# Layer 3's head normalisation as tensor_scalar pieces on two engines in a new order of tasks, and another path for the softmax denominators of layers 0 to 2

## The chip, the cores and the metric

The kernel runs on one core of one Trainium2 chip. The metric is the device time of one execution in microseconds (us), taken as the median of several runs. PE, DVE, ACT and POOL are the engines TensorE, VectorE, ScalarE and GpSimd; SP issues the DMAs.

## The reference, cut to what matters

The reference is a network of four layers on x (16 batches of 128 tokens, 256 wide) with a context of the same shape. Each layer is an attention and then a feed-forward part. The attentions of layers 0 to 2 differ in projections and heads (16 of width 8, 8 of width 16, 32 of width 8), but each is

```
scores = q @ k / sqrt(width)
prob   = softmax(scores, axis=-1)
out    = prob @ v            # the division by the softmax's sum may come last
```

Layer 3's attention has two passes: tokens over themselves ("own") and tokens over the context ("cross"). Each has 16 query heads and 8 key and value heads of width 128. Queries and keys are normalised head by head before the scores:

```
mu  = mean(x, -1); var = mean(square(x - mu), -1)
x   = (x - mu) * rsqrt(var + EPS) * w + b
```

and the concatenated output is rounded to FP8 values before the output projection.

## The kernel before, in words

The stages run one after the other: attention of layer 0 (`a0`), its feed-forward, attention of layer 1 (`a1`), and so on. The engines of a stage are separate programs that meet only at semaphores, and each runs its own list in program order.

**Attentions of layers 0 to 2** (class `Attention`, names `a_...` in the profile). The scores are computed twice from bf16 stacks `qs` and `ks`: `pe_first` (L326) gives them to `dve_max` (L476), which takes the row maxima; `pool_split` (L432 to L439), a turn on PE (L372) and a DMA (L513) put the maxima into reserved rows of the stack; `pe_second` (L344) gives scores less maximum to ScalarE's exponential (`act_exp`, L383). `pe_apply` (L361) multiplies by the values. The value tile has a column of ones behind each head's columns, so that PSUM row `HD` of each block of 32 rows holds the softmax's denominator. ScalarE copies a bank to `osb` (L412). Work is ordered by ticks: in tick g every engine does what `pair_at(g, offset)` and `batch_at(g, offset)` give it; two batches are a pair of 2W ticks (16, 8 and 8 in layers 0, 1 and 2). The tail of pair q is counted from `DONE`: at DONE the SP queue stores `osb` with all its 32 rows per block to DRAM (`od`, L517); at DONE+4 it waits for that and gathers the denominators (`zc`, L522) and the outputs (`oc`, L525, four DMAs or in layer 1 two); at DONE+7 VectorE takes the reciprocal (L482) and SP stores it (`zd`, L531); at DONE+9 SP spreads it (`zr`, L536); at DONE+12 GpSimd multiplies (`on`, L424); then PE projects in layers 0 and 2 (L701, L1035), and VectorE adds to X (L771, L902, L1092).

At a stage's start VectorE clears the stacks with memsets (`dve_clear`, L458, L461), and GpSimd presets `edge`, `mx` and `vt` (`pool_preset`, L444 to L449) ahead of all its ticks. Layer 0's VectorE program then has its constants (L743 to L755), whose last result (`bias_ready`) PE awaits before its first projection. SP's `sp_edges` waits for the clearing, and the stack DMAs (L502, L507) stand behind it in SP's queue.

**Layer 3** (class `Layer3Pass`; `a3o_` own, `a3x_` cross). Every engine runs its tasks of one list, `OWN_ORDER` or `CROSS_ORDER`, per batch. A step works on four batches at once: "a" attends, "c" centres and turns the heads, "p" projects, "r" prepares the next. A batch has 24 heads of 128 elements. ScalarE copies projections to `raw` (L2705), VectorE takes `bn_stats` (L2801) and derives mean and variance (`deviation`, L2807 to L2818), GpSimd raises to the power -1/2 (`inverse`, L2517, L2519) and centres the heads in six units of four (`center`): one 128x512 subtraction of a broadcast mean (L2525), a drain, one 128x512 multiplication (L2529). PE turns a unit (`turn_heads`, L2615) after the semaphore `centered`. VectorE also has the maxima of the scores (L2822), `normalise` (L2826, L2829), the rounding of the output (`round_task`, L2242 to L2246, L2838, L2842) and, in the own pass, the rounding of the input.

Of the kernel before, what the change touches and what calls it, by code (L numbers as in the profile page):

```python
# [12 lines left out]
F32 = mybir.dt.float32  # L13
# [9 lines left out]
P = 128  # L23
# [147 lines left out]
class Attention:  # L171
# [5 lines left out]
    def __init__(self, nc, st, X, name, heads, width, n, halves, scale, lead, stacks, values):  # L177
# [38 lines left out]
        self.od = nc.dram_tensor(f"{name}_od", (B // 2, 4, 32, G * 2 * D), F32, kind="Internal").ap()  # L216
# [7 lines left out]
        self.cleared = sem("cleared")  # L224
# [54 lines left out]
    def stacks_in(self, engine, q, dmas):  # L279
        engine.wait_ge(self.stack_in[q % self.SB], 16 * dmas * (q // self.SB + 1))  # L280
# [120 lines left out]
    def act_outputs(self, act, b, i):  # L401
        act.wait_ge(self.av_done, self.QUADS * b + (i + 1) * self.BANK_QUADS)
        q = b // 2
        if q >= 2 and b % 2 == 0 and i == 0:
            act.wait_ge(self.od_in, 16 * (q - 1))
# [14 lines left out]
    def pool_divide(self, pool, q):  # L420
        pool.wait_ge(self.zr_in[q % 2], 16 * (q // 2 + 1))
        pool.wait_ge(self.oc_in[q % 2], 16 * self.G * (q // 2 + 1))
        wait(pool, self.added, q)
        self.nc.gpsimd.tensor_tensor(self.on[:, :, :], self.oc[:, q % 2, :, :], self.zr[:, q % 2, :, :],  # L424
                                     ALU.mult).then_inc(self.on_ready, 1)

    def pool_split(self, pool, b):
# [3 lines left out]
        wait(pool, self.turned, b)  # L431
        self.nc.gpsimd.tensor_copy(self.mx[:, :, :, 0, :], raw).then_inc(self.split_step, 1)  # L432
# [9 lines left out]
    def pool_preset(self, pool):  # L442
        nc = self.nc
        nc.gpsimd.memset(self.edge[:, 0, :], 0.0).then_inc(self.preset, 1)  # L444
        nc.gpsimd.memset(self.edge[:, 1, :], -1.0).then_inc(self.preset, 1)
        nc.gpsimd.memset(self.mx[:, :, :, :, :], 0.0).then_inc(self.preset, 1)
# [38 lines left out]

    def sp_edges(self, sp):

        if self.HALVES == 1:
            sp.wait_ge(self.cleared, 1)
            return  # L490
        sp.wait_ge(self.cleared, 2)
        sp.wait_ge(self.preset, 2)
        out = self.maxima_slots(self.ks[:, :, :, :, :]).rearrange("p s t b n -> p (s t) (b n)")
        sp.dma_start(out, self.edges(1, out)).then_inc(self.edge_in, 16)

    def edges(self, k, out):
        return self.edge[0:8, k, :].unsqueeze(1).broadcast_to(list(out.shape))

    def sp_clear_maxima(self, sp, q):

        out = self.maxima_slots(self.qs[:, q % self.SB, :, :, :]).rearrange("p t b n -> p t (b n)")
# [13 lines left out]
    def sp_store_outputs(self, sp, q):  # L515
        sp.wait_ge(self.o_taken, 2 * self.QUADS // self.BANK_QUADS * (q + 1))
        sp.dma_start(self.od[q].rearrange("j r n -> (j r) n"), self.osb[:, q % 2, :, :, :]).then_inc(self.od_in, 16)  # L517

    def sp_gather_outputs(self, sp, q):
        sp.wait_ge(self.od_in, 16 * (q + 1))  # L520
        wait(sp, self.zd_in, 16 * (q - 1))
        sp.dma_start(self.zc[0:32 * self.G, q % 2, :], self.od[q, :, self.HD]).then_inc(self.z_in, 16)  # L522
        wait(sp, self.on_ready, q - 1)
        for k in range(self.G):
            sp.dma_start(self.oc[k:P:self.G, q % 2, :, :].rearrange("p b n -> p (b n)"),  # L525
                         self.od[q, :, 0:self.HD, 2 * k * D:2 * k * D + 2 * D].rearrange("j d n -> d j n")
                         ).then_inc(self.oc_in[q % 2], 16)

# [4 lines left out]
    def sp_spread_reciprocal(self, sp, q):  # L533
        sp.wait_ge(self.zd_in, 16 * (q + 1))
        rows = 4 * self.G
        sp.dma_start(self.zr[:, q % 2, :, :], self.zd[q].rearrange("(h n) -> h n", n=2 * D).unsqueeze(0).broadcast_to(  # L536
            [P // rows, rows, 2 * D])).then_inc(self.zr_in[q % 2], 16)
# [16 lines left out]
def stage_l0_attention(nc, dram, X):  # L554
    with Stage(nc, "a0") as st:
# [29 lines left out]
        with nc.Block() as block:  # L585
# [24 lines left out]
            def _(pool):  # L610
                a.pool_preset(pool)
                for g in a.ticks():
                    if (b := a.batch_at(g, LEAD + W)) is not None:
# [26 lines left out]
                    if (q := a.pair_at(g, DONE + 12)) is not None:  # L640
# [92 lines left out]
            def _(dve):  # L733
                a.dve_clear()

# [21 lines left out]
                dve.wait_ge(a.preset, a.presets())  # L757
                for g in a.ticks():
# [7 lines left out]
                    if (q := a.pair_at(g, DONE + 7)) is not None:  # L766
# [8 lines left out]
def stage_l1_attention(nc, dram, X):  # L775
    with Stage(nc, "a1") as st:
# [8 lines left out]
        with nc.Block() as block:  # L785
# [24 lines left out]
            def _(pool):  # L810
                a.pool_preset(pool)
                for g in a.ticks():
                    if (b := a.batch_at(g, LEAD + W)) is not None:
# [17 lines left out]
                    if (q := a.pair_at(g, DONE + 12)) is not None:  # L831
# [74 lines left out]
def stage_l2_attention(nc, dram, X):  # L906
    with Stage(nc, "a2") as st:
# [20 lines left out]
        with nc.Block() as block:  # L928
# [2109 lines left out]
```

## Time and profile before

| | |
|---|---|
| median of 3 runs | 3255.49 us (3253.8 to 3255.79) |
| the profiled execution | 3247.69 us, its span 3245.9 us |
| PE, DVE, ACT, POOL busy | 74%, 58%, 41%, 34% of the span |
| attention of layer 0 | about 16 to 349 us of the span |
| attention of layer 1 | about 514 to 705 us |
| attention of layer 2 | about 1064 to 1308 us |
| layer 3, own and cross | about 1547 to 2170 and to 2701 us |

Times of rows are microseconds from the span's start. A busy share is an average over stages with different limits; the waits within a stage say what sets its pace.

### The profile page before, as it was taken

Reading aid. Unit: us, or ns where it says so; the run is one execution under the profiler, and the core shown is the slowest. Engines: PE = TensorE matmul, PEld = TensorE weight load, DVE = VectorE, ACT = ScalarE, POOL = GpSimd, SP = SyncE. Lnnn points to the kernel's source line nnn. Section 1 sums busy time; section 2 is a strip of 40 time slices with the busy share of each in tenths; the row PEclk is TensorE's granted clock in tenths of the full one; section 3 lists DMA queues with packets and bytes.
Section 4 is the critical chain, followed back from the end, with each engine's and each line's share of the span. In section 5 each row is a group of like instructions: output and inputs, shape, how many; then the busy total and the mean of one; then the engine's idle time right before and its main releaser. Section 6 shows DMA issues by size and latency. Waiting matters only on the chain. (4 is left out here: it accounts for less than half of the span.)

```text
span 3245.9 us, 45398 instructions
## 1 busy us (share of the span) xinstructions
PE 2403.6 (74%) x14854; PEld 1747.9 (54%) x14906; DVE 1870.1 (58%) x3551; ACT 1324.1 (41%) x3059; POOL 1102.8 (34%) x991
## 2 busy tenths in 40 slices
PE   3887143855988477499278788867888984899997
PEld 2332021423556333477166666646777764778776
DVE  3775586645453354333588888857788775332332
ACT  0666151730200155111367667656666761111110
POOL 5432004510002342210367667527656650500000
PEclk9999565986989688599699999989999996899999
DMA  3342102522300234100200000020000001200001
GB/s 88 93 112 84 47 0 77 146 87 97 154 7 1 72 103 135 49 4 1 92 1 0 0 0 0 1 73 5 4 5 3 4 1 63 65 1 1 1 1 26
DMA packets 83598, 138.04 MB, mean 43 GB/s; under 512 B 19760, under 2 KB 63216, under 8 KB 78192
## 3 DMA queue, kind: packets, MB, share of 16 engines
q1 hardware_dynamic: 83440, 135.99, 13.4%
q8 instruction: 92, 1.51, 0.2%
q14 instruction: 66, 0.54, 0.1%
HBM read 76.64 MB, written 23.72 MB: 31 GB/s over the span
## 5 line engine op out<-in xcount | busy, mean ns | idle before, releaser
L476 DVE TENSOR_REDUCE a_mraw<-a_first_ps 128x4 f32<-128x1024 f32 (+1 forms) x256 | 309.2, 1220 | 126.4 <-PE a_first_ps L326 126.1
L383 ACT ACTIVATE a_et<-a_second_ps 128x1024 f32<-128x1024 f32 x256 | 262.4, 1025 | 160.1 <-PE a_second_ps L344 158.2
L1425 DVE TENSOR_TENSOR f3e_gated<-f3e_silu,f3e_u_ps 128x512 f32<-128x512 f32 x96 | 66.0, 687 | 305.4 <-PE f3e_s_ps L1376 203.3
L1406 ACT ACTIVATE f3e_silu<-f3e_g_ps 128x512 f32<-128x512 f32 x96 | 57.4, 598 | 397.4 <-PE f3e_g_ps L1363 397.4
L1385 PE MATMUL f3e_y_ps<-f_w,f3e_hidden 128*128 128x256 f32 x768 | 181.4, 380 | 1.9
L361 PE MATMUL a_o_ps<-a_et,a_vt 128*32 128x256 f32 x2048 | 167.6, 400 | 10.4 <-ACT a_osb L412 9.0
L344 PE MATMUL a_second_ps<-a_qs,a_ks 64*128 64x256 bf16 (+2 forms) x896 | 117.4, 297 | 58.6 <-ACT a_et L383 54.6
L1385 PEld LDWEIGHTS f3e_y_ps<-f_w,f3e_hidden 128*128 128x128 f32 x768 | 146.6, 191 | 18.4 <-DVE f3e_hidden L1428 1.2
L326 PE MATMUL a_first_ps<-a_ks,a_qs 64*128 64x256 bf16 (+2 forms) x1280 | 122.5, 266 | 32.1 <-DVE a_mraw L476 17.7
L2655 PE MATMUL a3o_o_ps<-a3o_wparts,a3o_catq 128*128 128x256 bf16 x768 | 111.0, 302 | 36.9 <-DVE a3o_catq L2842 36.5
L344 PEld LDWEIGHTS a_second_ps<-a_qs,a_ks 64*128 64x128 bf16 (+1 forms) x896 | 42.1, 96 | 157.8 <-ACT a_et L383 123.5
L2525 POOL TENSOR_TENSOR a3o_raw<-a3o_raw,a3o_mu 128x512 f32<-128x512 f32 x96 | 120.7, 1258 | 4.0 <-issue 2.7
L2696 ACT ACTIVATE a3x_weights<-a3x_s_ps,a3x_nmax 128x128 f32<-128x128 f32 x256 | 91.4, 379 | 63.0 <-DVE a3x_nmax L2822 63.0
L2529 POOL TENSOR_TENSOR a3x_raw<-a3x_raw,a3x_dev 128x512 f32<-128x512 f32 x96 | 111.1, 1157 | 14.3 <-issue 1.5
L2525 POOL TENSOR_TENSOR a3x_raw<-a3x_raw,a3x_mu 128x512 f32<-128x512 f32 x96 | 112.5, 1171 | 4.4 <-issue 3.2
L2655 PEld LDWEIGHTS a3o_o_ps<-a3o_wparts,a3o_catq 128*128 128x128 bf16 x768 | 80.6, 109 | 60.3 <-DVE a3o_catq L2842 45.3
L2529 POOL TENSOR_TENSOR a3o_raw<-a3o_raw,a3o_dev 128x512 f32<-128x512 f32 x96 | 105.0, 1094 | 13.6
L1345 POOL CAST f_w_high<-f_w_raw 128x512 fp32r<-128x512 f32 x36 | 25.0, 695 | 237.2 <-SPq L1324 218.9
L326 PEld LDWEIGHTS a_first_ps<-a_ks,a_qs 64*128 64x128 bf16 (+1 forms) x1280 | 70.9, 100 | 60.2 <-DVE a_mraw L476 26.7
L2696 ACT ACTIVATE a3o_weights<-a3o_s_ps,a3o_nmax 128x128 f32<-128x128 f32 x256 | 92.0, 388 | 27.6 <-DVE a3o_nmax L2822 26.8
L2577 PE MATMUL a3x_p_ps<-a_wkv,a3x_ctx_parts 128*128 128x512 f32 x384 | 102.9, 411 | 0.0
L2655 PE MATMUL a3x_o_ps<-a3x_wparts,a3x_catq 128*128 128x256 bf16 x768 | 96.8, 277 | 7.6 <-DVE a3x_catq L2842 7.6
(540 smaller groups left out, 6564.8 us busy)
## 6 DMA issues: line engine op xcount, KB each, us to landing
f_w<-in_f_w SPq DMA_DIRECT2D x16, 1216.0 KB, 8.7
a_qs<-a_parts SPq DMA_DIRECT2D x144, 128.0 KB, 2.4
a_od<-a_osb SPq DMA_DIRECT2D x16, 1024.0 KB, 3.9
a_ks<-a_parts SPq DMA_DIRECT2D x96, 128.0 KB, 2.5
f_w_raw<-in_f_w SPq DMA_DIRECT2D x25, 256.0 KB, 2.7
a_zr<-a_zd SPq DMA_DIRECT2D x24, 256.0 KB, 3.7
a_oc<-a_od SPq DMA_DIRECT2D x64, 64.0 KB
a_od<-a_osb SPq DMA_DIRECT2D x8, 512.0 KB, 3.3
```

What stands on the lines that cost most here:

```text
L326: last = nc.tensor.matmul(self.first_ps[:, g % 2, u, c * N:c * N + N], self.queries(p, self.ROWS, b, tq, rows), self.keys(p, self.ROWS, b, ...
L344: last = nc.tensor.matmul(out, self.keys(p, self.ROWS_WITH_MAXIMA, b, t, rows), self.queries(p, self.ROWS_WITH_MAXIMA, b, tq, slice(0, N)) ...
L361: last = nc.tensor.matmul(self.o_ps[32 * j:32 * j + 32, columns], self.vt[:, b // 2 % self.NV, b % 2, c, self.block(k, j), :], self.et[:, ...
L383: self.nc.scalar.activation(self.et[:, g % self.WAVES_HELD, :, :], self.second_ps[:, :, :], ACT.Exp, scale=self.scale).then_inc(self.e_rea ...
L476: v.tensor_reduce(out, self.first_ps[:, g % 2, :, :].rearrange("p u (c n) -> p u c n", n=N), AX.X, ALU.max).then_inc(self.max_taken, 1)
L1385: last = nc.tensor.matmul(y_ps[:, k, 0:D], hidden[:, t % 2, k * P:k * P + P], self.w2[:, t, :], start=(t == 0), stop=(t == L - 1))
L1425: nc.vector.tensor_tensor(gated[:, t % 2, :], silu[:, t % 2, :], u_ps[:, :], ALU.mult).then_inc(gated_ready, 1)
L2525: nc.gpsimd.tensor_tensor(heads, heads, mu[:, 4 * r:4 * r + 4].unsqueeze(2).broadcast_to([P, 4, HEAD]), ALU.subtract)
L2529: nc.gpsimd.tensor_tensor(heads, heads, dev[:, 4 * r:4 * r + 4].unsqueeze(2).broadcast_to([P, 4, HEAD]), ALU.mult).then_inc(centered, 1)
L2577: mm = nc.tensor.matmul(out, lhs, rhs, start=(i == 0), stop=(i == len(pairs) - 1))
L2655: mm = nc.tensor.matmul(o_ps[:, 0:D], catq[:, u % 2, h, :], wparts[:, p, 4 * u + h, :], start=(u == 0 and h == 0 and p == 0), stop=(u == U ...
L2696: mm = nc.scalar.activation(weights[:, u % 2, h, :], s_ps[:, h, :], ACT.Exp, bias=nmax[:, u % 2, h:h + 1], accum_out=total[:, u % 2, h:h + 1])
```

## The change

Layer 3: `center` issues four `tensor_scalar` instructions of 128x128 (subtract, then multiply, mean and inverse deviation as per-partition scalars) in place of two `tensor_tensor` of 128x512 and a drain. Units 1 and 4 of the own pass and unit 2 of the cross pass go to VectorE (`center_here`), which waits for a new semaphore `dev_ready`. Both lists of tasks are new.

Layers 0 to 2: the denominators go from `osb` straight to `zc` at DONE, ahead of the store. In layers 0 and 2 (`COMPACT`) only the rows that hold outputs are stored, in four DMAs, loaded back by one, and the reciprocals are spread by four; the columns of the projection behind are permuted to suit. The reciprocal moves to DONE+4, the gathering to DONE+6, the spreading to DONE+7, the multiplication to DONE+13. VectorE's clearing goes; small DMAs from `edge` fill the rows that need it, and the bulk of GpSimd's presets moves behind its first normalisations (tick 4 in layer 0, tick 1 in layers 1 and 2). The first `SB` pairs no longer clear the maxima rows in SP's queue.

```diff
@@ Attention
+        self.COMPACT = halves == 2
+        self.OD_STORES, self.OC_LOADS, self.ZR_LOADS = (4, 1, 4) if self.COMPACT else (1, G, 1)
...
-    def dve_clear(self):
-        if self.HALVES == 1:
-            self.nc.vector.memset(self.ks[96:P, :, :, :, :], -1.0).then_inc(self.cleared, 1)
-            return
-        for stack in (self.ks, self.qs):
-            self.nc.vector.memset(stack[:, :, :, :, :].bitcast(F32), 0.0).then_inc(self.cleared, 1)
...
     def sp_edges(self, sp):
+        sp.wait_ge(self.preset, 2)
+        sp.dma_start(self.maxima_slots(ks), self.edges(1, self.maxima_slots(ks))).then_inc(self.edge_in, 16)
+        if self.HALVES == 2:
+            sp.dma_start(ks[14:P:16], self.edges(0, ks[14:P:16])).then_inc(self.edge_in, 16)
+            for rows in (ks[7:P:8], qs[6:P:8], qs[7:P:8]):
+                sp.dma_start(rows, self.edges(0, rows)).then_inc(self.edge_in, 16)
...
     def sp_store_outputs(self, sp, q):
         sp.wait_ge(self.o_taken, 2 * self.QUADS // self.BANK_QUADS * (q + 1))
+        wait(sp, self.zd_in, 16 * (q - 1))
+        sp.dma_start(self.zc[0:32 * self.G, q % 2, :],
+                     self.osb[self.HD:P:32, q % 2, :, :, :].rearrange("j g b n -> j (g b n)")).then_inc(self.z_in, 16)
+        if self.COMPACT:
+            for j in range(4):
+                sp.dma_start(self.od[q, j], self.osb[32 * j:32 * j + self.HD, q % 2, :, :, :]).then_inc(self.od_in, 16)
...
     def sp_outputs(self, sp, g):
         if (q := self.pair_at(g, self.DONE)) is not None:
             self.sp_store_outputs(sp, q)
         if (q := self.pair_at(g, self.DONE + 4)) is not None:
+            self.sp_store_reciprocal(sp, q)
+        if (q := self.pair_at(g, self.DONE + 6)) is not None:
             self.sp_gather_outputs(sp, q)
         if (q := self.pair_at(g, self.DONE + 7)) is not None:
-            self.sp_store_reciprocal(sp, q)
-        if (q := self.pair_at(g, self.DONE + 9)) is not None:
             self.sp_spread_reciprocal(sp, q)
...
@@ Layer3Pass
+    OWN_HERE, CROSS_HERE = (1, 4), (2,)
...
                     def center(b, m):
                         r = self.TURN_ORDER[m]
-                        heads = raw[:, parity(b), 4 * r:4 * r + 4, :]
-                        nc.gpsimd.tensor_tensor(heads, heads,
-                                                mu[:, 4 * r:4 * r + 4].unsqueeze(2).broadcast_to([P, 4, HEAD]),
-                                                ALU.subtract)
-                        nc.gpsimd.drain()
-                        nc.gpsimd.tensor_tensor(heads, heads,
-                                                dev[:, 4 * r:4 * r + 4].unsqueeze(2).broadcast_to([P, 4, HEAD]),
-                                                ALU.mult).then_inc(centered, 1)
+                        for h in range(4 * r, 4 * r + 4):
+                            head = raw[:, parity(b), h, :]
+                            mm = nc.gpsimd.tensor_scalar(head, head, mu[:, h:h + 1], dev[:, h:h + 1],
+                                                         ALU.subtract, ALU.mult)
+                        mm.then_inc(centered, 1)
...
+                    def center_here(b, m):
+                        dve.wait_ge(dev_ready, at_batch(b, 1, 1))
+                        r = self.TURN_ORDER[m]
+                        for h in range(4 * r, 4 * r + 4):
+                            head = raw[:, parity(b), h, :]
+                            mm = v.tensor_scalar(head, head, mu[:, h:h + 1], dev[:, h:h + 1], ALU.subtract, ALU.mult)
+                        mm.then_inc(centered_here, 1)
```

In the new own list the vector engine's order is: maximum 0, rows, normalise 0, maximum 1, statistics 0, centre here 1, normalise 1, statistics 1, maximum 2, input rounding, statistics 2, normalise 2, maximum 3, centre here 4, round 0, normalise 3, round 1, statistics 3, round 2, round 3, statistics 4 and 5, deviation, add. GpSimd's is: centre 0, centre 2, quantise, centre 3, centre 5, inverse. Before, VectorE had statistics 0 to 2 and rounds 0 and 1 spread among six centres of GpSimd.

## Rows read from the trace of the kernel before

**Rows 1.** Windows, steady stretches of own and cross: engines' busy us, clock, DMA.
```profile
1800.00:1834.40 34.40, 27.96 (x176) 22.72 (x174) 29.63 (x71) 23.43 (x74) 22.84 (x17) 0.95 0.00 0
2400.00:2431.00 31.00, 27.52 (x179) 22.94 (x178) 25.27 (x66) 21.39 (x68) 19.07 (x16) 1.00 0.02 4
```
**Rows 2.** By source line, final addition: ns min/median/max, first and last start.
```profile
L2846 DVE SCALAR_TENSOR_TENSOR X<-a3o_o_ps,a3o_out_scale,X x16: 476/483/484, 1668.7 to 2170.1; 128x256 f32 x12, 128x256 f32<-128x256 f32 x4
L2846 DVE SCALAR_TENSOR_TENSOR X<-a3x_o_ps,a3x_out_scale,X x16: 477/484/485, 2246.2 to 2700.5; 128x256 f32 x12, 128x256 f32<-128x256 f32 x4
```
**Rows 3.** Instruction groups, DVE, own pass: busy us, mean ns, idle before.
```profile
L2244 DVE TENSOR_SCALAR a3o_cexponent<-a3o_cat 128x512 int16<-128x512 int16 x64 | 62.7, 979 | 4.8
L2842 DVE TENSOR_TENSOR a3o_catq<-a3o_cat,a3o_cmagic 128x512 bf16<-128x512 bf16 x64 | 52.8, 824 | 4.8
L2838 DVE TENSOR_TENSOR a3o_cat<-a3o_cat,a3o_cmagic 128x512 bf16<-128x512 bf16 x64 | 42.5, 664 | 4.8
```
**Rows 4.** By source line, the same operations: ns min/median/max, own pass.
```profile
L2244 DVE TENSOR_SCALAR a3o_cexponent<-a3o_cat x64: 293/969/2081, 1645.5 to 2166.9; 128x512 int16<-128x512 int16 x64
L2838 DVE TENSOR_TENSOR a3o_cat<-a3o_cat,a3o_cmagic x64: 424/426/1701, 1647.8 to 2167.6; 128x512 bf16<-128x512 bf16 x64
```
**Rows 5.** Instruction groups, POOL, own pass: the two halves of centring.
```profile
L2525 POOL TENSOR_TENSOR a3o_raw<-a3o_raw,a3o_mu 128x512 f32<-128x512 f32 x90 | 112.4, 1249 | 3.8 <-issue 2.7
L2529 POOL TENSOR_TENSOR a3o_raw<-a3o_raw,a3o_dev 128x512 f32<-128x512 f32 x90 | 98.6, 1096 | 12.8
```
**Rows 6.** Timeline and source line: tensor_scalar with two per-partition scalars, POOL and DVE.
```profile
531.07 2.46 POOL L417 TENSOR_SCALAR a_xn<-X,a_mean,a_rstd 128x256 f32<-128x256 f32 x2
L2790 DVE TENSOR_SCALAR a3o_xs<-X,a_mean,a_rstd x16: 403/404/1128, 1563.0 to 2044.4; 128x256 f32 x12, 128x256 f32<-128x256 f32 x4
```
**Rows 7.** Timeline, start of layer 0's attention: start us, duration us.
```profile
19.43 0.52 POOL L444 MEMSET a_edge<- 128x512 bf16 x1 [0.72 <-POOLq L43]
...
32.30 0.23 DVE L743 TENSOR_SCALAR a_freq<-a_freq,a_sign 128x256 f32<-128x256 f32 x1
```
**Rows 8.** Timeline, start of layer 1's attention.
```profile
528.79 13.71 DVE L458 MEMSET a_ks<- 32x16384 bf16 x1 [7.36 <-issue]
...
537.69 2.12 POOL L829 TENSOR_TENSOR a_parts<-a_rest,a_parts 128x1024 bf16<-128x1024 f32 x1 [1.16 <-ACT a_parts L882]
...
542.53 0.64 SPq L507 DMA_DIRECT2D a_qs<-a_parts  x1
```
**Rows 9.** Timeline, start of layer 2's attention.
```profile
1082.06 0.59 ACT L1055 COPY a_xt<-a_m_ps 128x512 f32<-128x512 f32 x1 [25.36 <-PE a_m_ps L1004]
```
**Rows 10.** Timeline, the last pair of layer 0.
```profile
331.87 0.32 SPq L517 DMA_DIRECT2D a_od<-a_osb  x1
335.66 0.55 SPq L522 DMA_DIRECT2D a_zc<-a_od  x1
...
338.04 0.55 DVE L482 RECIPROCAL a_zc<-a_zc 128x64 f32<-128x64 f32 x1 [6.63 <-DMA a_zc<-a_od]
...
345.13 1.26 POOL L424 TENSOR_TENSOR a_on<-a_oc,a_zr 128x512 f32<-128x512 f32 x1 [20.25 <-DMA a_zr<-a_zd]
```
**Rows 11.** Timeline, the last pairs of layers 1 and 2.
```profile
691.35 0.33 SPq L517 DMA_DIRECT2D a_od<-a_osb  x1
...
703.07 1.26 POOL L424 TENSOR_TENSOR a_on<-a_oc,a_zr 128x512 f32<-128x512 f32 x1 [6.30 <-DMA a_zr<-a_zd]
...
1288.53 0.33 SPq L517 DMA_DIRECT2D a_od<-a_osb  x1
...
1302.25 1.26 POOL L424 TENSOR_TENSOR a_on<-a_oc,a_zr 128x512 f32<-128x512 f32 x1 [6.06 <-DMA a_zr<-a_zd]
```
**Rows 12.** Timeline, within layers 0 and 1: a late denominator, a late division.
```profile
205.33 0.55 DVE L482 RECIPROCAL a_zc<-a_zc 128x64 f32<-128x64 f32 x1 [2.44 <-DMA a_zc<-a_od]
...
209.22 1.02 ACT L383 ACTIVATE a_et<-a_second_ps 128x1024 f32<-128x1024 f32 x1 [2.40 <-PE a_second_ps L344]
...
615.97 1.63 DVE L902 TENSOR_TENSOR X<-X,a_on 128x512 f32<-128x512 f32 x1 [1.98 <-POOL a_on L424]
```

More of the change, by code:

```diff
@@ L279, in stacks_in @@
     def stacks_in(self, engine, q, dmas):
-        engine.wait_ge(self.stack_in[q % self.SB], 16 * dmas * (q // self.SB + 1))
+        first = 1 if self.HALVES == 2 else 0
+        engine.wait_ge(self.stack_in[q % self.SB], 16 * (dmas * (q // self.SB + 1) - first))
     def max_rows_in(self, engine, b):
@@ L313, in pe_first @@
         g = self.W * b + w
-        if g == 0 and self.HALVES == 2:
-            pe.wait_ge(self.edge_in, 16)
+        if g == 0:
+            pe.wait_ge(self.edge_in, 16 * (self.EDGES if self.HALVES == 2 else 1))
         if w == 0 and b % 2 == 0:
@@ L482, in dve_reciprocal, with edges, sp_clear_maxima @@
         self.nc.vector.reciprocal(self.zc[0:rows, q % 2, :], self.zc[0:rows, q % 2, :]).then_inc(self.z_ready, 1)
+    EDGES = 5
     def sp_edges(self, sp):
-        if self.HALVES == 1:
-            sp.wait_ge(self.cleared, 1)
-            return
[L491 to L499, printed above, removed]
+        ks = self.ks[:, :, :, :, :].rearrange("p s t b n -> p (s t) (b n)")
+        qs = self.qs[:, :, :, :, :].rearrange("p s t b n -> p (s t) (b n)")
+        sp.wait_ge(self.preset, 2)
[4 more added lines that the diff above has]
+                sp.dma_start(rows, self.edges(0, rows)).then_inc(self.edge_in, 16)
+    def edges(self, k, out):
+        return self.edge[0:out.shape[0], k, :].unsqueeze(1).broadcast_to(list(out.shape))
+    def sp_clear_maxima(self, sp, q):
+        if q < self.SB:
+            return
         out = self.maxima_slots(self.qs[:, q % self.SB, :, :, :]).rearrange("p t b n -> p t (b n)")
@@ L534, in sp_spread_reciprocal @@
         sp.wait_ge(self.zd_in, 16 * (q + 1))
-        rows = 4 * self.G
-        sp.dma_start(self.zr[:, q % 2, :, :], self.zd[q].rearrange("(h n) -> h n", n=2 * D).unsqueeze(0).broadcast_to(
-            [P // rows, rows, 2 * D])).then_inc(self.zr_in[q % 2], 16)
+        wait(sp, self.on_ready, q - 1)
+        if self.COMPACT:
+            for j in range(4):
+                row = self.zd[q].rearrange("(j n) -> j n", j=4)[j:j + 1]
+                sp.dma_start(self.zr[32 * j:32 * j + 32, q % 2, :, :], row.broadcast_to([self.HD, row.shape[1]])
+                             ).then_inc(self.zr_in[q % 2], 16)
+        else:
+            rows = 4 * self.G
+            row = self.zd[q].rearrange("(h n) -> h n", n=2 * D).unsqueeze(0)
+            sp.dma_start(self.zr[:, q % 2, :, :], row.broadcast_to([P // rows, rows, 2 * D])
+                         ).then_inc(self.zr_in[q % 2], 16)
     def sp_outputs(self, sp, g):
@@ L2336 @@
         ("a", "scores", 0), ("a", "exponential", 0), ("a", "maximum", 0), ("c", "project values", 0),
-        ("c", "keep values", 0), ("c", "center", 0), ("a", "maximum", 1), ("c", "project values", 1),
-        ("c", "keep values", 1), ("a", "scores", 1), ("a", "normalise", 0), ("a", "exponential", 1),
[15 rows of a table removed]
+        ("c", "keep values", 0), ("a", "normalise", 0), ("c", "center", 0), ("c", "project values", 1),
+        ("r", "value", 0), ("a", "scores", 1), ("a", "maximum", 1), ("c", "keep values", 1), ("a", "turn", 0),
+        ("a", "exponential", 1), ("c", "center here", 2), ("p", "project", 0), ("p", "keep", 0),
[14 rows of a table added]
     ]
@@ L2365, in run @@
         ORDER = self.OWN_ORDER if own else self.CROSS_ORDER
+        HERE = self.OWN_HERE if own else self.CROSS_HERE
+        THERE = tuple(m for m in range(self.LN_UNITS) if m not in HERE)
         with Stage(nc, self.name) as st:
@@ L2430, in run @@
             var_ready = sem("var_ready")
+            dev_ready = sem("dev_ready")
             centered = sem("centered")
+            centered_here = sem("centered_here")
             heads_turned = sem("heads_turned")
```

107 lines of the change are left out of this document (63 added, 44 removed), and 47 rows, old and new, of tables (CROSS_ORDER, OWN_ORDER).

## The prediction

> **What bounds the kernel now.** I began with the page's busy shares and slices: no engine is full over the span, and the stages differ. So I took the change stage by stage: windows for how full each engine is, the addition that closes each batch for its period, then instruction groups, and for the starts and tails the timeline.
>
> Layer 3. The 16 closing additions give (2170.1-1668.7)/15 = 33.4 us a batch in the own pass and (2700.5-2246.2)/15 = 30.3 in the cross pass [rows 2]. In 34.4 us of the own pass DVE is busy for 29.6, PE for 28.0, POOL for 22.8; in 31.0 us of the cross pass PE for 27.5, DVE for 25.3 [rows 1]. So DVE sets the own pass, PE nearly sets the cross pass. But much of DVE's time is no work: the exponent step of the rounding takes 293 ns at best and 979 on average, an addition of the rounding 424 at best and 664 on average, the subtraction behind it, of the same size, 824 [rows 3, 4]. With four roundings a batch these three lose 4 x (0.69+0.24+0.40) = 5.3 us a batch. They lose it while POOL's centring runs, whose instructions take 1.25 and 1.10 us [rows 5]: each waits about one POOL instruction.
>
> Layers 0 to 2. Each start is serial, each tail is a chain of DMAs, and in between a late denominator holds DVE and with it the maxima.
>
> **The change: layer 3.** *POOL.* A unit costs now 1.25+1.10 = 2.35 us [rows 5]. A tensor_scalar with two per-partition scalars takes 2.46/2 = 1.23 us on 256 elements [rows 6]; on 128 no row shows it. Bounds: half of that (0.62) and all of it. I take 0.70, near the half, since POOL's time per element dominates. A unit of four becomes 2.8 us (bounds 2.5 and 4.9), dearer by 0.45. The own pass keeps 4 units, 11.2 against 14.1; the cross pass 5, 14.0 against 14.1 at the same prices. POOL has 11 us idle in its window [rows 1], so its total matters only through DVE and PE.
>
> *DVE.* The same operation takes 0.404 us on 256 elements at the median and 1.128 at worst [rows 6]. On 128 it lies between 0.20 and 0.40 alone; I take 0.22 from start to start, 0.88 a unit. So DVE gains 1.75 us of work a batch in the own pass and 0.88 in the cross pass. The worst case shows that it can wait for POOL too: if all four wait for 0.7 each, a unit costs 2.8 or more.
>
> *Their meetings.* What DVE loses is about a POOL instruction at each meeting, and that shrinks from 1.1 or 1.25 to 0.7, by 40%; there is also a fifth less centring in the own pass, and rounds 2 and 3 now come after POOL's last unit. The loss of 5.3 falls to 5.3 x 0.6 x 0.8 = 2.5; I take half of a possible 1.5 us of new waits of the pieces. Own: +1.75-2.8+0.75 = -0.3 of DVE's busy time. The other three contended operations of the rounding and normalising lie outside these rows; their share makes it about -0.7.
>
> *Order.* DVE's unit waits for `dev_ready`; behind it stand normalise 1, statistics and the maxima that ScalarE's exponentials need. In the own list six DVE tasks precede it (add, maximum 0, rows, normalise 0, maximum 1, statistics 0), more than the inverse's span, so I cost this wait at nothing; without that cover it would be 1 to 2 us a batch. PE's turn of the unit stands far behind. Of the 34.4 us, DVE idles 4.8 [rows 1]; the list puts maxima ahead of roundings, so that exponentials run beside roundings. I take 1.0 of the idle time back. Own: -1.7 us a batch (floor: PE's 28.0 of 34.4, so at most -5.5; above: +3 if the pieces wait). Cross: PE's idle 3.5 of 31.0 limits the gain; half as much moves, so -0.8. Over 15 periods each: -25.5 and -12, together **-38** (bounds -110 and +65).
>
> By the Trainium skill, "SBUF — State Buffer", section "Who interferes with whom", GpSimd and a two-port or two-input Vector instruction take the shared port pair for a whole instruction and the first to start wins. By that rule shorter GpSimd instructions shorten every wait, and the rows agree (293 ns alone, 979 on average). The same section lets `tensor_scalar` contend; the result that this gives is the third rival.
>
> **The change: layers 0 to 2.**
>
> *Starts.* Layer 0: DVE's constants begin at 32.30, behind two memsets; without them they can begin just after the block does, at 19.43 [rows 7], so near 19.8: -12.5. POOL's long memset moves between its normalisations and the first addition, 12 us later, and is hidden there. Layer 1: SP's first stack DMA goes at 542.53, when the 13.7 us memset ends, though the data end at 537.69+2.12 = 539.8 [rows 8]: -3 (POOL's presets move, but stand ahead of those data either way). Layer 2: ScalarE still awaits all presets before its copy at 1082.06 [rows 9], and they end now only some 0.3 earlier: -0.2. The edge DMAs, five of some 0.7 us of issue, stand in SP's queue well before the first stack DMA; if they land late, 3 to 5 us of each start are lost.
>
> *Tails.* Layer 0's last pair: store 331.87, gather 335.66, reciprocal 338.04, division 345.13 [rows 10]. A small copy took 338.04-335.66 = 2.4 us, so denominators are there at 334.3, not 338.0: 3.7 earlier. Against it stand four spreading DMAs for one, up to three issues of 0.6 later, each smaller: -3. Layer 1 (691.35 to 703.07) and layer 2 (1288.53 to 1302.25) [rows 11]: the store's landing leaves the chain in the same way, -3.4 and -3.5. Together -10.
>
> *Within.* DVE waits 2.44 us for the denominators at 205.33 and the exponential at 209.22 is 2.40 late where 0.5 is usual [rows 12]; layer 0 has five such pairs: 5 x 1.9 less something for what is late next (PE's shared bank), -8. Layer 1: DVE waits 1.98 for the division and its addition takes 1.63 at 615.97 [rows 12]; the reciprocal path is two ticks earlier, the division one tick later, behind POOL's subtractions instead of before them: three pairs of about 2, -6. Layer 2 waits elsewhere: -1. SP issues 11 DMAs of tail for 8 in layers 0 and 2, some 1.8 us more a pair, ahead of the DMA of maxima; I cost this at nothing, since stores come a tick before that and SP idles between; else +1 a pair.
>
> Sum: -15.7-10-15 = **-41** (bounds -50 and -15).
>
> Together -79: 3247.69-79 = 3169 for the profiled execution. The median stands 7.8 above that execution, so 3255.5-79 = 3176. I forecast **3175**.
>
> **The rivals.**
>
> 1. *DVE freed, PE the bound.* Roundings no longer meet centring and the new lists close the idle time: own -4 a batch, cross -1.6, 15 each: -84, with -41 in all 3255.5-125 = **3130**. For it: the loss is real and PE is busy only 28 of 34.4 [rows 1]. Against: DVE gets 1.75 us more, POOL's unit is dearer.
> 2. *Layer 3 doesn't move.* What shorter meetings give, the new pieces take: only -41, **3214**. For it: total POOL time in the cross pass is the same.
> 3. *The pieces wait (the other side).* Each DVE piece waits for a POOL piece and DVE's queue stands behind it: a unit costs 2.8 to 4 us where I took 0.88, twice in an own batch and once in a cross batch, with the maxima behind it. It decides from 41/15 = 2.7 us more per own and cross period together. With own +3 and cross +1.5: +68-41 = +27, **3282**. For it: the 1128 ns at worst [rows 6]. Against: its median is 404.
> 4. *The denominators' path does not do what it says*: stores from 8 partitions or edge fills land late, and half of the -41 is lost: 3175+20 = **3195**.
>
> **How the numbers follow.** Forecast 0.40 (3155 to 3197 its own range), rival 1 0.25, rival 2 0.18, rival 3 0.08, rival 4 0.09. The range 3112 to 3232 takes in all but rival 3 and the ends of 1. This kernel's measurement can tell 0.2%, 6.5 us, from no change. Faster 0.90, same 0.03, slower 0.07.
>
> **What would show it.** Own period near 31.7 and cross near 29.5 between closing additions; the exponent step's mean from 979 to near 600 ns; DVE pieces near 0.25 and POOL pieces near 0.70; DVE's constants in layer 0 near 19.8; no wait of DVE for the denominators in layer 0; division about 10 us behind the last store in each tail. DVE pieces at 0.9 us and an own period above 34 would refute it; so would first waves that wait for edges.

## The result, and the profile after

The changed kernel takes **3119.49 us** (median of 4 runs, 3118.72 to 3123.46) against 3254.64 (4 runs, 3250.29 to 3255.79): ratio 0.959, 95% interval 0.9573 to 0.9606, or 135 us less, where 80 were forecast. The profiled execution took 3118.86 us, its span 3117.0 (before 3245.9).

First the closing additions of layer 3, by source line, as in [rows 2]:
```profile
L2886 DVE SCALAR_TENSOR_TENSOR X<-a3o_o_ps,a3o_out_scale,X x16: 478/484/488, 1645.3 to 2100.0; 128x256 f32 x12, 128x256 f32<-128x256 f32 x4
L2886 DVE SCALAR_TENSOR_TENSOR X<-a3x_o_ps,a3x_out_scale,X x16: 476/483/484, 2177.4 to 2575.9; 128x256 f32 x12, 128x256 f32<-128x256 f32 x4
```
The own period is (2100.0-1645.3)/15 = 30.31 us for 33.43, the cross period (2575.9-2177.4)/15 = 26.57 for 30.29: 46.7 and 55.8 us over 15 periods each, together 102.5 of the 128.9 us between the two spans, four fifths. Windows of one period, with the columns of [rows 1] (two own, one cross):
```profile
1780.00:1810.30 30.30, 25.89 (x162) 21.00 (x161) 24.43 (x75) 22.86 (x73) 22.76 (x21) 0.94 0.00 0
1810.30:1840.60 30.30, 26.67 (x177) 21.98 (x177) 26.50 (x80) 23.95 (x78) 23.14 (x22) 1.00 0.00 0
2300.00:2326.60 26.60, 26.58 (x178) 22.75 (x177) 21.51 (x69) 21.23 (x69) 22.55 (x24) 1.00 0.02 5
```
In the cross pass PE is busy for 26.58 of 26.60 us: it is the bound there. In the own pass no engine is full; which chain of waits sets its 30.31 us was not followed up. The instruction groups of DVE and POOL that answer to [rows 3, 5]:
```profile
L2857 DVE TENSOR_SCALAR a3o_raw<-a3o_raw,a3o_mu,a3o_dev 128x128 f32<-128x128 f32 x128 | 68.2, 600 | 0.2 <-POOL a3o_dev L2551 0.2
L2878 DVE TENSOR_TENSOR a3o_cat<-a3o_cat,a3o_cmagic 128x512 bf16<-128x512 bf16 x64 | 30.3, 473 | 4.8
L2882 DVE TENSOR_TENSOR a3o_catq<-a3o_cat,a3o_cmagic 128x512 bf16<-128x512 bf16 x64 | 27.5, 430 | 4.8
L2558 POOL TENSOR_SCALAR a3o_raw<-a3o_raw,a3o_mu,a3o_dev 128x128 f32<-128x128 f32 x256 | 232.0, 917 | 4.8 <-issue 4.8
```
And by source line, minimum, median and maximum, the exponent step of [rows 4], POOL's pieces and DVE's:
```profile
L2270 DVE TENSOR_SCALAR a3o_cexponent<-a3o_cat x64: 293/296/385, 1632.7 to 2096.7; 128x512 int16<-128x512 int16 x64
L2558 POOL TENSOR_SCALAR a3o_raw<-a3o_raw,a3o_mu,a3o_dev x256: 785/872/2785, 1591.2 to 2058.7; 128x128 f32<-128x128 f32 x128
L2857 DVE TENSOR_SCALAR a3o_raw<-a3o_raw,a3o_mu,a3o_dev x128: 329/372/2246, 1594.8 to 2055.7; 128x128 f32<-128x128 f32 x128
```
The exponent step is never longer than 385 ns, where its median was 969. POOL's pieces are longer than forecast (872 for 700), DVE's too (372 at the median, 600 on average), and still DVE is busy for less than before: 24.4 and 26.5 of 30.3 us.

In layers 0 to 2 less came than forecast. From the first instruction of each attention's stage to its last addition: layer 0's end moved from 348.62 to 329.87 (-18.8), layer 1's stage from 190.1 to 179.5 (-10.6), layer 2's from 243.0 to 247.1 (**+4.1**), in all -25. The additions of layers 0 and 2, by source line, each with the idle time of DVE ahead of it (us in total, times):
```profile
L797 DVE SCALAR_TENSOR_TENSOR X<-a_m_ps,a_bm,X x8: 751/752/753, 142.2 to 329.9; 128x512 f32<-128x512 f32 x8
...
  PE a_m_ps L730: 43.4, 8
L1118 DVE TENSOR_TENSOR X<-X,a_m_ps x8: 686/687/689, 1183.1 to 1287.8; 128x512 f32<-128x512 f32 x8
...
  PE a_m_ps L1063: 41.0, 8
```
Before, DVE was idle for 32.0 and 25.0 us ahead of these additions. It waits longer now, for the output projection behind POOL's division. In layer 0, though, 32.1 of the 43.4 us (before, 24.6 of the 32.0) stand ahead of the last two additions, where DVE has no maxima left; within the stage the wait grew from 7.4 to 11.3 us.

### The profile page after: what moved, and what is told of

Its sections match the earlier page's. It is cut to its first block and busy times, and to the rows that moved or that the text cites. A ratio compares the mean times of both kernels' runs of the same rounds, so it can differ in the third digit from the quotient of the medians.

```text
span 3117.0 us, 45806 instructions
## 1 busy us (share of the span) xinstructions
PE 2380.8 (76%) x14906; PEld 1740.0 (56%) x14906; DVE 1739.0 (56%) x3738; ACT 1320.1 (42%) x3059; POOL 1169.4 (38%) x1183
## 5 line engine op out<-in xcount | busy, mean ns | idle before, releaser
L2558 POOL TENSOR_SCALAR a3x_raw<-a3x_raw,a3x_mu,a3x_dev 128x128 f32<-128x128 f32 x320 | 281.7, 892 | 5.3 <-issue 5.3
L2558 POOL TENSOR_SCALAR a3o_raw<-a3o_raw,a3o_mu,a3o_dev 128x128 f32<-128x128 f32 x256 | 232.0, 917 | 4.8 <-issue 4.8
L2549 POOL TENSOR_TENSOR a3o_dev<-a3o_var,a3o_minus_half 128x24 f32<-128x24 f32 x16 | 69.0, 4310 | 94.8 <-DVE a3o_var L2850 94.8
L1362 POOL CAST f_x_high<-f_xnt 128x1024 fp32r<-128x1024 f32 x9 | 9.3, 1038 | 252.7 <-PE f3e_s_ps L1402 175.1
L2687 PE MATMUL a3o_o_ps<-a3o_wparts,a3o_catq 128*128 128x256 bf16 x768 | 101.9, 286 | 0.6 <-DVE a3o_catq L2882 0.6
L2606 PE MATMUL a3o_p_ps<-a_wq,a3o_xq 128*128 128x512 f32 x256 | 80.6, 441 | 27.5 <-ACT a3o_vv L2743 16.8
```

The source lines that it names most:

```text
L2549: nc.gpsimd.tensor_tensor(dev[:, :], var[:, :], minus_half[:, :], ALU.pow)
L2558: mm = nc.gpsimd.tensor_scalar(head, head, mu[:, h:h + 1], dev[:, h:h + 1], ALU.subtract, ALU.mult)
L2606: mm = nc.tensor.matmul(out, lhs, rhs, start=(i == 0), stop=(i == len(pairs) - 1))
L2687: mm = nc.tensor.matmul(o_ps[:, 0:D], catq[:, u % 2, h, :], wparts[:, p, 4 * u + h, :], start=(u == 0 and h == 0 and p == 0), stop=(u == U ...
```

## The experiments

Times from different chips are compared by their ratio to the kernel before. A step of 0.001 is 3.25 us.

| kernel | layer 3: order / POOL's centring / division | ratio | 95% interval | us |
|---|---|---|---|---|
| e1 | changed; layers 0 to 2 as before | 0.9659 | 0.9642 to 0.9675 | 3142.0 |
| e2 | old / two wide / no | 0.9925 | 0.9909 to 0.9942 | 3230.0 |
| e8 | new / two wide / no | 0.9980 | 0.9968 to 0.9991 | 3244.3 |
| e6 | new / two wide / yes | 0.9940 | 0.9918 to 0.9961 | 3233.1 |
| e12 | old / two, by head / no | 0.9854 | 0.9839 to 0.9869 | 3205.7 |
| e7 | new / two, by head / yes | 0.9634 | 0.9618 to 0.9650 | 3131.5 |
| e5 | old / pieces / no | 0.9768 | 0.9752 to 0.9785 | 3178.0 |
| e4 | new / pieces / no | 0.9788 | 0.9771 to 0.9804 | 3180.3 |
| e3 | old / pieces / yes | 0.9694 | 0.9678 to 0.9711 | 3154.0 |
| changed | new / pieces / yes | 0.9590 | 0.9573 to 0.9606 | 3119.5 |
| e10 | changed, quantisation in pieces too | 0.9605 | 0.9592 to 0.9618 | 3123.6 |
| e9 | changed, additions of layers 0, 2 later | 0.9546 | 0.9533 to 0.9559 | 3102.9 |
| e11 | e9, quantisation in 256 columns | 0.9520 | 0.9507 to 0.9533 | 3095.4 |

From e2 on, all have layers 0 to 2 as changed. "Two wide" is the old subtraction and multiplication of 128x512; "pieces" one `tensor_scalar` a head.

**Which half gave what: e1 and e2.** The edit is the change's layer 3, or its attentions of layers 0 to 2, alone.

> Layer 3 as changed (pieces, division, order), the attentions of layers 0 to 2 as before. Theory A (the traces' sum: layer 3 gave about 110 us, the layers ahead of it about 20): 3254.6 - 110 = 3145 us, 3138 to 3152. Rival B (the prediction's terms: layer 3 gave 38 and layers 0 to 2 gave 41, and what is left came from the two together, for instance from a later stage that meets other transfers): 3217 us or more.

> The attentions of layers 0 to 2 as changed, layer 3 as before. Theory A: 3254.6 - 20 = 3235 us, 3229 to 3240. Rival B, the prediction's term of 41 us: 3214 us.

Layer 3 alone takes off 112.0 us, the rest alone 24.0. They add up to the whole (136 of 135): theory A in both. The forecast had 38 and 41.

**Form, division and order: e3, e5, e4, e6, e8.** e3 puts the old lists back, with `center here` at the old places of units 1, 4 (own) and 2 (cross). e5 and e4 undo the division:
```
-    OWN_HERE, CROSS_HERE = (1, 4), (2,)
+    OWN_HERE, CROSS_HERE = (), ()
```
and the units stand in rising order. e6 and e8 give POOL its old form back, for four units and for six.

> The changed kernel with layer 3's two orders as they were before, the pieces and the division between GpSimd and VectorE kept (the units that VectorE takes stand at their old places). Theory A (the one-input form takes the load from VectorE's own operations, and that is what layer 3 gained): most of the 110 us stay, 3120 to 3150 us. Rival B (the order gave it; the form alone moves only where the idle time lies): 3200 to 3240 us. In between, 3150 to 3200, each has a share.

> The changed kernel with the old orders and all six units on GpSimd by pieces: of the change in layer 3 only the form is left. Theory A: VectorE's five slowed operations run as fast as in the changed kernel (the exponent's 0.98 us falls to about 0.31), GpSimd does 24 pieces of about 0.9 us = 22 us a batch, which fits in 30: 3130 to 3165 us. Rival B (order): 3200 to 3240 us, with the exponent's operation fast and VectorE idle instead. Rival C (GpSimd's pieces, 24 in a row, come late for TensorE): over 3235 us, TensorE's transposes wait for raw.

> The changed kernel, new orders, all six units on GpSimd by pieces (24 pieces of about 0.9 us a batch, 22 of 30 us). The division was worth 24 us in the old orders. Theory A (it spares GpSimd a third of its centring and brings those units earlier to TensorE, in any order): 3119 + 24 = 3143, 3130 to 3165. Rival B (the new orders were made so that it matters little, or VectorE, freed of its 12 pieces, gains what GpSimd loses): 3112 to 3125.

> The changed kernel with GpSimd's units as before, two tensor_tensor of 512 columns each (subtract, then multiply), order and division kept. Theory A (the two-input form on GpSimd is what slows VectorE's two-byte operations): the exponent's operation back near 0.9 us, and the time up by at least the 52 us that the form alone gave in the old orders, 3160 to 3200. Rival B (the division and order give the gain whatever the form): 3115 to 3130 us, the exponent's operation at about 0.3 us.

> New orders alone in layer 3: GpSimd's two wide tensor_tensor for all six units, no division. With layers 0 to 2 changed and layer 3 as before the time is 3230. Theory A (the order alone does little, since VectorE stays slowed): 3215 to 3235. Rival B (the order is worth its 34 us by itself): 3190 to 3205. Rival C (the order was made for short units and is worse with long ones): over 3240.

One way through the cube: the form alone -51 us (0.9925 to 0.9768), then the division -24 (0.9694), then the order -34 (0.9590). Another way: the order alone **+18** (0.9980), the division -13 (0.9940), the form -114 (0.9590). So the order costs 18 us with GpSimd's wide form and no division (e8, rival C's outcome), makes no clear difference with pieces and no division (e5 and e4, whose intervals overlap), and gives 34 us with pieces and division. Old order, wide form and division together were not run. The expectations that took a share as fixed were all missed: e3 came 4 us above A's range, e5 between A and B, e4 15 us above A's range, since the division is worth 64 us in the new order, and e6 33 us above A's. In e6 DVE's loss is also elsewhere than I expected: the exponent step takes 458 ns on average, not 0.9 us, but DVE's own pieces and the weights stand beside POOL's wide instructions now:
```profile
L2860 DVE TENSOR_SCALAR a3o_raw<-a3o_raw,a3o_mu,a3o_dev 128x128 f32<-128x128 f32 x128 | 99.1, 834 | 0.1
L2872 DVE TENSOR_TENSOR a3o_weights<-a3o_weights,a3o_inv_total 128x512 f32<-128x512 f32 x64 | 69.4, 1085 | 4.8
```
The order moves the meetings, it doesn't end them. In e3, the old order with pieces and division, the exponent step still takes 646 ns on average and 2087 at worst, beside GpSimd's quantisation, while DVE's pieces take 358; in the new order it is the pieces that meet the quantisation (600) and the step that is free (308). Why the division is worth so much, a window of an own period of e5 shows:
```profile
1806.00:1838.00 32.00, 25.74 (x169) 21.48 (x170) 22.64 (x68) 24.29 (x75) 29.58 (x30) 1.00 0.00 0
```
Six units of pieces fill POOL for 29.58 of 32.0 us, and TensorE's turns wait for it: 54.0 us in the own pass, for 3.6 before.
```profile
L2647 PE MATMUL a3o_t_ps<-a3o_ident,a3o_raw 128*128 128x128 f32 x384 | 61.3, 284 | 54.0 <-POOL a3o_raw L2558 53.9
```
The pieces free DVE and bind POOL; the division then unloads POOL. Most of the gain needs both.

**Length or form: e7 and e12.** The edit keeps two inputs and cuts the instruction:
```
+                        for h in range(4 * r, 4 * r + 4):
+                            head = raw[:, parity(b), h, :]
+                            nc.gpsimd.tensor_tensor(head, head, mu[:, h:h + 1].broadcast_to([P, HEAD]), ALU.subtract)
+                        nc.gpsimd.drain()
...
```


> As the kernel of the two wide tensor_tensor, but each cut into four of 128 columns, so that GpSimd issues eight short instructions of two inputs for a unit. Theory A (two inputs at once, not the length of the instruction, slow VectorE): as slow as with the wide ones or slower, 3160 to 3220 us, the exponent's operation at 0.8 us or more. Rival B (a short instruction lets VectorE in between): the exponent's operation falls to 0.3 to 0.5 us and the time to 3120 to 3140.

> Layers 0 to 2 changed; in layer 3 the old orders, no division, and GpSimd's two two-input operations of 512 columns cut into eight of 128: nothing is changed but the length of an instruction. Layer 3 as before gives 3230, all six units by one-input pieces 3178. Theory A (the length is what costs): 3175 to 3200, the exponent's operation of the own pass from 0.98 us to below 0.5. Rival B (in the new order the short pieces helped by where they fell, not by their length): 3220 or more, the exponent's operation above 0.7 us. Rival C (eight starts a unit make GpSimd the bound): DVE fast, TensorE waiting for raw, 3200 to 3230.

e7 is rival B's outcome: the cut alone, with the same work and eight instructions for two, takes 0.9940 to 0.9634, 99 us of the 114 that the one-input form took. So the two inputs as such were not the main cost; the length of the instruction was. The exponent step of the own pass by source line in e6 (wide), e7, e12 and e5:
```profile
L2270 DVE TENSOR_SCALAR a3o_cexponent<-a3o_cat x64: 293/294/1106, 1637.4 to 2168.6; 128x512 int16<-128x512 int16 x64
```
```profile
L2270 DVE TENSOR_SCALAR a3o_cexponent<-a3o_cat x64: 293/329/469, 1637.3 to 2111.7; 128x512 int16<-128x512 int16 x64
```
```profile
L2270 DVE TENSOR_SCALAR a3o_cexponent<-a3o_cat x64: 293/330/469, 1634.1 to 2148.8; 128x512 int16<-128x512 int16 x64
```
```profile
L2270 DVE TENSOR_SCALAR a3o_cexponent<-a3o_cat x64: 293/302/380, 1634.1 to 2131.7; 128x512 int16<-128x512 int16 x64
```
POOL's own instructions in e7, beside which DVE's waited at most 469-293 = 176 ns:
```profile
L2558 POOL TENSOR_TENSOR a3o_raw<-a3o_raw,a3o_mu x256: 389/400/2246, 1595.6 to 2072.2; 128x128 f32<-128x128 f32 x128
L2562 POOL TENSOR_TENSOR a3o_raw<-a3o_raw,a3o_dev x256: 392/410/1377, 1599.1 to 2074.1; 128x128 f32<-128x128 f32 x128
```
Beside the pieces of `tensor_scalar`, twice as long, the step waited at most 380-293 = 87 ns in e5 (92 in the changed kernel). So the wait doesn't simply follow the length of POOL's instruction: beside wide two-input ones of 1.04 to 1.09 us it is up to 1106-293 = 813 ns (e6), beside `tensor_scalar` pieces a tenth of one. What the rest of a piece is spent on, no run shows. In e12 POOL is nearly as full as in e5 (29.77 of 33.0 us), and TensorE's turns wait 60.0 us for it: the time misses A's range by 6 us and lies in rival C's, with C's mechanism. e12 and e5 don't hold all else equal, however. In the trace before, 13 of the 64 exponent steps of the own pass stand beside GpSimd's quantisation, in e5 and e12 none does; POOL waits there 37.0 and 36.6 us for the quantisation's input, for 81.0 before, which fits a fuller POOL that comes to it later. So 51 and 23 us in the old order are length or form together with this shift. e6 and e7, where no exponent step meets the quantisation, are the clean pair.

**The instructions that stayed wide: e10.** In the changed kernel all 36 instructions of DVE in the own pass that take over 0.3 us more than the best of their kind stand beside POOL's quantisation. The timeline, start and duration:
```profile
1810.33 2.13 POOL L2565 TENSOR_TENSOR a3o_value<-a3o_value,a3o_magic 128x1024 bf16<-128x1024 bf16 x1
1810.39 0.16 DVE L2866 RECIPROCAL a3o_inv_total<-a3o_total 128x4 f32<-128x4 f32 x1
1810.63 2.38 DVE L2869 TENSOR_TENSOR a3o_weights<-a3o_weights,a3o_inv_total 128x512 f32<-128x512 f32 x1
...
1813.50 1.65 POOL L2571 TENSOR_TENSOR a3o_xq<-a3o_value,a3o_magic 128x768 fp32r<-128x768 bf16 x1
1813.53 1.70 DVE L2857 TENSOR_SCALAR a3o_raw<-a3o_raw,a3o_mu,a3o_dev 128x128 f32<-128x128 f32 x1
```
The weights' 0.69 us become 2.38 and end 0.5 us behind POOL's 2.13 (1810.63+2.38 = 1813.0, against 1812.5); a piece of 0.33 takes 1.70 and ends with POOL's 1.65. The same step's reciprocal, with one small input, takes 0.16 us beside it. e10 cuts the quantisation into 16 instructions of 128 columns:
```
+                            for k in range(4):
+                                for c in range(2):
+                                    nc.gpsimd.tensor_tensor(value16[:, k, c, :], value16[:, k, c, :], magic[:, k, c, :],
+                                                            ALU.add)
```


> The changed kernel with GpSimd's three remaining wide two-input operations of the own pass (1024 columns 2.14 us, 256 columns 0.75, 768 columns 1.64) cut into pieces of 128 columns, 16 a batch. Theory A (a VectorE operation that wants what GpSimd's instruction holds waits to the end of that one instruction, so that the length of GpSimd's instruction is the price, not its form): VectorE's pieces of raw fall from 600 ns on average to about 380 (their longest from 2246 to below 700), weights from 860 to about 730, some 2.4 us of 30.3 a batch; with TensorE the next bound 10 to 25 us come off, 3095 to 3110. Rival B (the slowing follows the share of time in which GpSimd reads two inputs, however it is cut): VectorE's durations as they are, and GpSimd's extra starts make it 3119 to 3130. Rival C: VectorE's durations fall, the time doesn't (TensorE bound or the chain through GpSimd's longer quantisation): 3116 to 3122.

DVE did what theory A says:
```profile
L2865 DVE TENSOR_SCALAR a3o_raw<-a3o_raw,a3o_mu,a3o_dev x128: 328/393/472, 1602.6 to 2061.2; 128x128 f32<-128x128 f32 x128
L2877 DVE TENSOR_TENSOR a3o_weights<-a3o_weights,a3o_inv_total x64: 691/693/923, 1630.8 to 2094.3; 128x512 f32<-128x512 f32 x64
```
but the time didn't move beyond the intervals (0.9605 for 0.9590): rival C, 2 us above its range. (It lies in rival B's range too, but B wanted DVE's durations unchanged.) The own period fell by 0.3 us only, to (2105.7-1656.1)/15 = 29.97, 5.1 us in 15 periods, and nearly as much went again at the start: the first addition comes 125.2 us into layer 3, where it came 120.3 in the changed kernel. The group of TensorE's turns names the new wait, 39.9 us for 7.1:
```profile
L2655 PE MATMUL a3o_t_ps<-a3o_ident,a3o_raw 128*128 128x128 f32 x384 | 58.7, 284 | 39.9 <-POOL a3o_raw L2558 39.9
```

**The additions' tick: e9.** In layers 0 and 2, for TensorE's projection and DVE's addition:
```
-                    if (q := a.pair_at(g, DONE + 14)) is not None:
+                    if (q := a.pair_at(g, DONE + 15)) is not None:
```


> The changed kernel with the output projection (TensorE) and the addition to X (VectorE) one tick later, at DONE + 15, in layers 0 and 2; the division of GpSimd stays at DONE + 13. Theory A (these layers gave 20 to 24 us where 41 were forecast since the division was moved from 12 to 13 and the addition of layer 2 from 15 to 14, so that VectorE waits at it: 43.4 us in all in layer 0 against 32.0 before, 41.0 against 25.0 in layer 2): the waits fall back and 6 to 12 us of 3119 come off, 3107 to 3114. Rival B (VectorE has slack there, and SP's queue, which issues 11 transfers for 8, holds the pairs up): 3117 to 3122, the waits shorter and the stages as long.

0.9590 to 0.9546, 14 to 17 us by either measure, a little more than A gave. Layer 0's last addition ends 10.8 us earlier. The waits at the addition fell little there in total (43.4 to 39.8), since most of them lie at the last two. But what ScalarE's exponentials wait for the second product fell by as much as the stage: after, then e9, by source line between 60 and 330 us:
```profile
L386 ACT ACTIVATE a_et<-a_second_ps x128: 1016/1023/1040, 80.7 to 310.7; 128x1024 f32<-128x1024 f32 x128
...
  PE a_second_ps L347: 75.1, 103
```
```profile
L386 ACT ACTIVATE a_et<-a_second_ps x128: 1017/1023/1036, 79.9 to 300.6; 128x1024 f32<-128x1024 f32 x128
...
  PE a_second_ps L347: 64.3, 106
```
The timeline shows the way. In TensorE's list the output projection stands ahead of the tick's second product, so a projection that waits for POOL's division holds ScalarE at once. One of the four alike pairs, after, then e9:
```profile
172.85 1.09 PE L730 MATMUL a_m_ps<-a_on,a_wm 128*128 128x512 f32 x2 [2.13 <-POOL a_on L428]
...
174.31 1.02 ACT L386 ACTIVATE a_et<-a_second_ps 128x1024 f32<-128x1024 f32 x1 [2.84 <-PE a_second_ps L347]
```
```profile
170.46 1.10 PE L730 MATMUL a_m_ps<-a_on,a_wm 128*128 128x512 f32 x2 [0.62 <-POOL a_on L428]
...
171.92 1.02 ACT L386 ACTIVATE a_et<-a_second_ps 128x1024 f32<-128x1024 f32 x1 [0.39 <-PE a_second_ps L347]
```
Over the four pairs ScalarE's idle time at this place is 11.9 us after the change and 1.6 in e9 (6.7 before the change): 10.3 of the 10.8 us. DVE's addition waits for the same projection (2.57, in e9 1.06 us) and holds the maxima behind it; what that alone costs is not shown, since e9 moves both. Layer 2's stage gained 3.2 us (247.1 to 243.9, where before it took 243.0).

**Both: e11.** e9, with the quantisation in pieces of 256 columns from the fourth batch on.

> The kernel with the later addition (3102.9 us), and GpSimd's quantisation of the own pass cut into pieces of 256 columns from the fourth batch on (7 a batch besides the one of 256 that stays; the first three batches keep the wide ones, since nothing of VectorE's runs beside them and their length is on the path into the loop). Theory A (pieces of 128 gave VectorE its 2.4 us a batch back and took as much on GpSimd by their starts, so that TensorE's transposes waited for GpSimd's raw, 39.9 us for 7.1; half as many pieces cost GpSimd half of that): 5 to 12 us below 3102.9, 3091 to 3098. Rival B (the own pass is bound by a chain in which GpSimd and VectorE stand one after the other, so that it is a trade at any size): 3100 to 3106.

7.5 us below e9, within A's range, though the intervals (0.9507 to 0.9533, 0.9533 to 0.9559) touch. Against e10 two things differ, the size of the pieces and the wide form in the first three batches, and they were not run apart; the first addition comes at 120.5 us of the layer again. The own period is 29.4 us (1632.5 to 2073.5 over 15), TensorE's turns wait 8.4. It is the fastest: 3095.4, 24 us under the change.

## Why the prediction was right, and where its sizes were off

The mechanism held and the time fell in the range, but the sum was short by 55 us, and its two halves were wrong in opposite directions. That the time fell in the range is partly luck: it lies 7 us inside the lower end, and with the forecast 41 us from layers 0 to 2 in place of the 24 measured it would have been 3102, outside. Rival 1, DVE freed and PE the bound, describes layer 3 better than the forecast did (it holds for the cross pass; in the own pass PE is not full), and even it was too small there (-84 for -112).

*Layer 3, -38 forecast, -112 measured (e1).* The mis-sized step is "their meetings". I let the loss of 5.3 us a batch shrink to 2.5 with the length of POOL's instruction. The three operations' means are now 308 (the group of the exponent step), 473 and 430 ns, or 4 x (0.015+0.049+0.006) = 0.3 us over their best. I assumed that a piece costs a whole piece's wait; e5 and the changed kernel show at most 92 ns for a piece of 872. That is why POOL's dearer pieces (0.87 for the 0.70 I took) did DVE no harm. A reading of the rows was wrong as well: I put the whole loss down to centring. In the trace before, about half of what the three operations lose (44 of 85 us in the own pass, counting each instruction by what POOL ran beside it longest) stands beside POOL's quantisation, which the change leaves as it was:
```profile
1827.87 2.12 POOL L2536 TENSOR_TENSOR a3o_value<-a3o_value,a3o_magic 128x1024 bf16<-128x1024 bf16 x1 [3.42 <-DVE a3o_magic L2246]
1828.07 2.07 DVE L2244 TENSOR_SCALAR a3o_cexponent<-a3o_cat 128x512 int16<-128x512 int16 x1
...
1831.00 1.81 POOL L2542 TENSOR_TENSOR a3o_xq<-a3o_value,a3o_magic 128x768 fp32r<-128x768 bf16 x1
1831.39 1.70 DVE L2842 TENSOR_TENSOR a3o_catq<-a3o_cat,a3o_cmagic 128x512 bf16<-128x512 bf16 x1
```
The worst case in [rows 4], 2081 ns, was the sign: 1.79 us of waiting is more than a centring instruction lasts. This half went because the new order takes the roundings away from the quantisation (e3, without it, keeps 42 us of it), which the forecast had no term for. By the Trainium skill, "SBUF — State Buffer", section "Who interferes with whom", the port pair that VectorE and GpSimd share goes to whichever issues first for its whole instruction, and the other is blocked; the trace agrees for wide two-input ones (2.38 beside 2.13), and for `tensor_scalar` pieces no wait of that length appears here.

*DVE's units, 0.88 us forecast for each.* 68.2 us over 32 units are 2.1, so 4.3 a batch for 1.75. At best a piece takes 0.33, not 0.22, and some meet the quantisation. Their waits come to 4.3-8x0.33 = 1.6 us a batch, for the 0.75 in the sum, and beside other instructions of POOL than rival 3 named.

*The other operations* that I valued at 0.4 gave more: the magic step (L2272) of the own pass went from 654 to 297 ns, of the cross pass from 724 to 308, the weights of the cross pass from 845 to 697.

*Cross pass, -0.8 forecast, -3.7 measured.* I took half of PE's idle time, and all of it went: 26.57 us are PE's own work. The window [rows 1] came near to it (27.52 busy of 31.0, in a period of 30.29: 26.9), and I used this floor as a limit only. The floor of the own pass had a slip: 28.0 us are PE's work in a window of 34.4, or 27.2 in a period of 33.4, so the limit was -6.2 and not -5.5.

*Order, 1.0 us forecast for the own batch.* It gives 34 us in all with the other two, and costs 18 without them. I costed the parts as if they could be added.

*`dev_ready`, nothing forecast:* DVE waited 0.2 us in 128 pieces. The cover named was enough.

*Layers 0 to 2, -41 forecast, -24 measured (e2).* Starts: DVE's constants in layer 0 at 19.61 for 32.30, its last one at 22.64 for 34.41, so -11.8 for -12.5; layer 1's first stack DMA stands 24.66 us into its stage for 28.24, -3.6 for -3; layer 2 -0.2, as forecast. Tails: from the first copy of the last pair to the division 11.7, 8.3 and 11.6 us for 13.3, 11.7 and 13.7 from the store before: -1.6, -3.4, -2.1 for -3, -3.4, -3.5. SP's timeline of layer 0's last pair shows what took the rest:
```profile
314.70 0.58 SPq L525 DMA_DIRECT2D a_zc<-a_osb  x1
315.32 2.62 SPq L529 DMA_DIRECT2D a_od<-a_osb  x4
317.99 0.85 SPq L549 DMA_DIRECT2D a_zd<-a_zc  x1
321.15 0.34 SPq L539 DMA_DIRECT2D a_oc<-a_od  x1
321.60 2.75 SPq L558 DMA_DIRECT2D a_zr<-a_zd  x4
```
Four stores for one stand before the denominators' store, and four spreading loads of 2.75 together behind the gather; I had counted the spreading alone. *Within*, -15 forecast, only -2.6 measured (-5.4, -3.6, +6.4): the step that failed. I priced the waits that go, and weighed the division's later tick in layer 1 alone; in layer 0 its projection and addition kept their tick, in layer 2 they moved one ahead. e9 gives 14 to 17 us back, which brings layers 0 to 2 to about the forecast 41. Still open is the rest in layer 2, whose exponentials span 146.5 us (145.5 in e9) for 142.2 before; SP's longer queue there was not tried alone.

*Rival 3* (pieces wait) and *rival 2* fell with the periods. *Rival 4* was near in size (20 us lost, 17 measured) and wrong in place: the starts came as forecast, and most of the loss was a tick's.

## What to carry to other kernels

Where VectorE's two-byte or two-input operations take far longer on average than at best, look at how long GpSimd's concurrent instructions are and where they fall, and cut these first: the cut gave here 99 us with the order and division, and 23 without them. Then ask what binds next (here GpSimd, whose short instructions cost more in all) and move a part of its work; test such edits together, since one alone can even cost. When a producer is moved a tick later, move its consumers as well: an engine runs its list in order, and what stands behind the waiting consumer is held too.

## What the runs showed of the hardware that was not expected

- GpSimd's `tensor_scalar` with two per-partition scalars on 128x128 f32 takes 785 ns at best, twice a `tensor_tensor` of that shape (389, in e7), which itself is above a quarter of the 128x512 one (1037/4 = 259, in the kernel before).
- GpSimd busy for 29.58 of 32.0 us, for the most part with such pieces (e5), leaves VectorE's exponent step at 293 to 380 ns.
- Cutting has a price on GpSimd: in the quantisation, pieces of 128 columns take 491 ns (value) and 641 (xq) on average, so that the two went from 2.2+1.6 us a batch to 3.7+3.7 (58.5 and 58.6 us busy over 16 batches); pieces of 256 take 729 and 740.
